# Adding the two parts of H by TensorE with two stacked unit matrices, and copying the sum by ScalarE, in a fused embedding and interaction kernel

## The reference, cut to what matters

```
# inp = e: [512, 32, 64]; W0: [128, 32*32], W1 and W2: [128, 64*32]
h = inp
for i, (W, b) in enumerate([(W0, b0), (W1, b1), (W2, b2)]):
    Wr = W.reshape(O, Hj, nf)
    nxt = einsum('bjk,bzk,ojz->bok', h, inp, Wr) + b[None, :, None]
    if i != n_layers - 1:
        h, o = nxt[:, :O // 2], nxt[:, O // 2:]
    else:
        o = nxt
    outs.append(o)
z = sum(concatenate(outs, axis=1), axis=2)
h = relu(concat([z, dense_ctx]) @ W_top1 + b_top1)
h = relu(h @ W_top2 + b_top2)
y = h @ W_top3
```

## Time and profile before

| | before |
|---|---|
| median of three executions | 665.0 us |
| the profiled execution's own time | 666.33 us |
| its span, first to last instruction | 664.6 us |
| mean granted TensorE clock | 0.977 of full speed |
| TensorE busy (matmuls / weight loads) | 627.3 us (94%) / 520.8 us (78%) |
| VectorE busy | 484.8 us (73%) |
| ScalarE busy | 213.1 us (32%) |
| GpSimd busy | 128.9 us (19%) |

### The profile page before, as it was taken

One profiled execution on the slowest core, in us unless ns is written; L12 is line 12 of the kernel. 1 busy time (PEld: TensorE's weight loads), 2 busy tenths in 40 slices (PEclk: granted clock), 3 DMA queues, 4 the chain that ended last, 5 costly groups with the idle time before them and its releaser, 6 DMA issues.

```text
span 664.6 us, 32262 instructions
## 1 busy us (share of the span) xinstructions
PE 627.3 (94%) x14488; PEld 520.8 (78%) x14488; DVE 484.8 (73%) x491; ACT 213.1 (32%) x351; POOL 128.9 (19%) x137
## 2 busy tenths in 40 slices
PE   5844899999999999999999999999999999999998
PEld 5833588888888888888888888888888888888773
DVE  4237788888888888888888888888888888851000
ACT  2330333444433333333333333333333333332012
POOL 7755044445443544100000000000000000000000
PEclk9686899999999999999999999999999999999999
DMA  5110011111111111100000000000000000002000
GB/s 180 30 28 17 14 24 28 28 25 32 26 25 24 29 26 27 20 15 13 12 12 12 12 12 12 12 12 12 12 12 12 12 12 12 12 18 65 11 1 0
DMA packets 31658, 14.87 MB, mean 22 GB/s; under 512 B 24177, under 2 KB 28897, under 8 KB 31378
## 3 DMA queue, kind: packets, MB, share of 16 engines
q1 hardware_dynamic: 27442, 10.26, 7.2%
q0 software_dynamic: 4192, 4.25, 2.9%
HBM read 8.03 MB, written 0.00 MB: 12 GB/s over the span
## 4 chain that ended last, share of the span: by engine, by line
PE 89%; POOL 5%; issue 3%; DVE 2%; DMA 1%; ACT 0%; DVEq 0%; POOLq 0%
PE psX L335 20%; PE psT L392 20%; PE psT L416 8%; PE psT L402 7%; PE psT L376 7%; PE psT L379 6%; POOL G_sb L239 5%; PE psX L379 4%; PE psX L376 4%; PE psX L346 3%; PE psX L466 2%; PE psX L355 1%; PE psX L273 1%; PE psT L480 1%; PE psX L496 1%
## 5 line engine op out<-in xcount | busy, mean ns | idle before, releaser
L392 PE MATMUL psT<-T_sb,W1d 64*64 64x256 f32 x1024 | 234.3, 379 | 0.0
L396 PE MATMUL psT<-T_sb,W1d 64*64 64x256 f32 x1024 | 234.3, 379 | 0.0
L402 PE MATMUL psT<-T_sb,W1d 64*64 64x256 f32 (+3 forms) x2048 | 205.3, 300 | 0.0
L684 DVE TENSOR_TENSOR prod<-X 128x1024 f32 (+4 forms) x202 | 170.7, 914 | 15.5 <-PE psT L379 15.3
L721 DVE STREAM_TRANSPOSE PT<-prod 128x4608 f32<-128x4608 f32 x32 | 159.0, 4969 | 0.0
L392 PEld LDWEIGHTS psT<-T_sb,W1d 64*64 64x64 f32 x1024 | 131.3, 133 | 27.8 <-issue 14.4
L335 PE MATMUL psX<-PT,W0T 32*64 32x256 f32 x4608 | 136.0, 382 | 12.5 <-DVE PT L721 9.1
L335 PEld LDWEIGHTS psX<-PT,W0T 32*64 32x64 f32 x4608 | 118.8, 134 | 32.9 <-issue 29.9
L416 PE MATMUL psT<-T_sb,W1d 64*64 64x64 f32 (+2 forms) x1536 | 141.7, 270 | 0.0
L396 PEld LDWEIGHTS psT<-T_sb,W1d 64*64 64x64 f32 x1024 | 131.3, 133 | 0.0
L402 PEld LDWEIGHTS psT<-T_sb,W1d 64*64 64x64 f32 x2048 | 123.6, 133 | 0.8
(11 more groups left out here) (78 smaller groups left out, 557.1 us busy)
## 6 DMA issues: line engine op xcount, KB each, us to landing
X<-T_sb SPq DMA_DIRECT2D x64, 64.0 KB, 2.0
kept<-grams SPq DMA_DIRECT2D x128, 16.5 KB
G_sb<-in_L_rec_W SPq DMA_DIRECT2D x2, 1024.0 KB, 4.8
E_q<-in_tbl,ids_g POOLq DMA_INDIRECT x96
prod<-in_W_top SPq DMA_DIRECT2D x2, 512.0 KB, 3.5
G_sb<-in_L_rec_W SPq DMA_DIRECT2D x1, 512.0 KB, 5.7
G_sb<-in_tbl,ids POOLq DMA_INDIRECT x32, 2.4
dT<-dT SPq DMA_DIRECT2D x3, 32.0 KB, 2.0
```

What stands on the lines that cost most here:

```text
L392: mm(psT[low, 0, 0:HF * SMP], W1d[low, HF + k, :], cross.rearrange("p v (z y) s -> p v z y s", y=HF)[:, :, :, k, :], start=start, stop=sto ...
L396: mm(psT[high, 0, 0:HF * SMP], W1d[low, k, :], T_flat[low, SMP * row:SMP * (row + HF)], start=start, stop=stop, tile_position=(0, C))
L402: last = mm(out[:, SMP * 4 * a:], W1d[high, HF * v + k, :], T_flat[high, SMP * (row + 4 * a):SMP * (row + HF)], start=start, stop=stop and ...
L684: return tt(out, x[:, :, z0:z0 + nz].unsqueeze(3).broadcast_to(shape), x[:, :, y0:y0 + ny].unsqueeze(2).broadcast_to(shape), ALU.mult)
```

## The change

TensorE makes 8 multiplies in place of the 16 transposes: the weights are all 128 rows by 128 columns of a tile of `H_sb`, the moving operand is `both`, two unit matrices of 64 x 64 one above the other. The product is the transposed sum of both parts, and lies in bank 0 of `psX`. ScalarE copies it to `H_T`, directly behind `h_copy`. VectorE's `ht_sum` is gone. VectorE makes `both` once at the start, and TensorE waits for it once. `b1_all` moves into a part of `G2_flat` that is free at that time.

```diff
+        both = sb("both", [P, C])
...
-        b1_all = sb("b1_all", [P, C])
...
+        b1_all = G2_flat[:, 7168:7168 + C]
...
             def h_transposes(m):
                 pe.wait_ge(h_evac, m + 1)
                 pe.sem_inc(turns, 1)
                 for t in range(TILES):
-                    for v in range(2):
-                        r = slice(C * v, C * v + C)
-                        last = nc.tensor.transpose(psX[:, v, C * t:C * t + C], H_sb[r, P * t:P * t + P], ident[r, r],
-                                                   tile_position=(C * v, 0))
+                    last = mm(psX[:, 0, C * t:C * t + C], H_sb[:, P * t:P * t + P], both[:, :], start=True, stop=True)
                 last.then_inc(h_tr, 1)
...
             h_matmuls(0)
+            pe.wait_ge(both_ready, 1)
             h_transposes(0)
...
+            def ht_copy(m):
+                act.wait_ge(h_tr, m + 1)
+                copy(H_T[:, :, :], psX[:, 0, :].rearrange("p (t o) -> p t o", o=C)).then_inc(ht_ready, 1)
...
             def step(n, lookups):
                 h_copy(n + 1)
+                ht_copy(n + 1)
...
             h_copy(0)
+            ht_copy(0)
             g0_copy(0)
...
             nc.vector.memset(kept[:, :, :, 0:NS:NS - 1], 0.0)
+            dve.wait_ge(identity, 2)
+            tt(both[:, :], ident[:, 0:C], ident[:, C:P], ALU.add).then_inc(both_ready, 1)
             nc.vector.memset(V_T[:, :, :], 0.0).then_inc(zeroed, 1)
...
-            def ht_sum(m):
-                dve.wait_ge(h_tr, m + 1)
-                nc.vector.tensor_reduce(H_T[:, :, :], psX[:, 0:2, :].rearrange("p v (t o) -> p t o v", o=C),
-                                        mybir.AxisListType.X, ALU.add).then_inc(ht_ready, 1)
...
             products(1, TILES)
-            ht_sum(0)
             dve.wait_ge(px_ready, 2)
...
                 products(e, dve.snap((n + 2) * TILES))
-                ht_sum(n + 1)
                 dve.wait_ge(px_ready, n + 3)
...
             t_copies(STEPS - 2)
-            ht_sum(STEPS - 1)
             add(STEPS - 2)
```

More of the change, by code:

```diff
@@ L138, in dlrm_tower @@
         ids0_in, idsg_in = sem("ids0_in"), sem("idsg_in")
-        identity = sem("identity")
+        identity, both_ready = sem("identity"), sem("both_ready")
         w0_sym = sem("w0_sym")
```

## The result

The changed kernel takes 700.8 us (median of four executions, 699.06 to 701.57) against 665.0 us before: the ratio is 1.054, with a 95% interval of 1.0509 to 1.0571. The forecast was 703.3 us, in a range of 694 to 714. The profiled execution took 699.06 us, its span is 697.3 us, 32.7 us above the span before.

A forecast was written before the change was run, and what follows sets the result against it. TensorE was taken to bound the steps. The terms 26.6 + 15.5 - 3.8 = +38.3 us on the profiled 666.33 gave 704.6, put on the median of the runs as 703.3 us; range 694 to 714.

The forecast's parts named there:

- The bound: In the steps TensorE is the bound; VectorE's sum is early by some 3.9 us, its transpose by 4.0 us.
- The rival by which VectorE sets the steps: VectorE's round is the longest, so removing 1.23 us from each of 32 gives 625.6 us; chance 0.01.
- 1. The multiplies: TensorE's stage at L346, paced like L469 at 0.121 us: 1.40 us per step without lookups, 1.29 with; 26.6 and 15.5 us.
- 2. ScalarE's copy at nothing: ScalarE's new 0.586 us copy falls into its idle time in each step, and nobody on TensorE or VectorE waits: cost 0.
- 3. The first step: Ahead of the loop VectorE's transpose no longer waits for its sum: 4.64 us gained, 0.81 lost before it, -3.8 in all.
- the drop of the clock goes with the stall: First step: without the 2.44 us wait at tile 5 the lower clock goes too; otherwise 2.2 us of gain are lost.
- The 0.77 us that the forecast left in place: A gap in L335 of the first step that nothing in the profile releases, expected to remain after the change.
- 4. Edits at nothing: Making `both` near the start is hidden by VectorE's wait for W0, and `b1_all` only changes its place: no cost.
- The one by which weight loads do not overlap in the whole array: At the stage no load runs beside the matmul before it: 15 loads of 0.203 us, total 743.9 us; chance 0.03.
- the one by which the moving columns alone set the pace: At L346 weights come in ahead of time, 16 pairs at 0.033 us each: 661.1 us, faster; chance 0.03.
- the half pace: Strides slow L469, and contiguous `both` runs at 0.066 us, the stage spans 0.99 us: 676.2 us; chance 0.07.

The follow-up runs named there:

- no_sum: The changed kernel with the 16 old transposes put back; ScalarE copies bank 0, so the second part of H is not added: 661.83 us, ratio 0.994.
- vector_copies: The changed kernel, but VectorE copies the sum to `H_T` at the place of its old reduction, and ScalarE does not: 703.18 us, ratio 1.0586.
- first_step_only: The kernel before, with multiplies by `both` and ScalarE's copy in the first step alone: 663.9 us, ratio 0.9979.
- held_first: The changed kernel, but VectorE's transpose ahead of the loop waits for `H_T` again: 703.10 us, against 701.35 for the unaltered changed kernel beside it.
- moving_32: The changed kernel with 32 instead of 64 moving columns in each multiply, half the outputs of H left out: 700.03 us, ratio 1.0531.

## Why the prediction was right, and where its terms were off

**The bound.** TensorE sets the steps, and VectorE's 1.23 us are worth nothing. This is shown by no_sum and vector_copies, in which the step without lookups stays within 0.01 us. The rival by which VectorE sets the steps is out.

**1. The multiplies.** This term carries the result, and its mechanism held: L469 was the right row to go by, and the loss is all in the stage. It was somewhat too high. The mean pace is 0.115 us and not 0.121, so 1.23 us and not 1.32; the exit is 430.40 - (428.48 + 1.725) = 0.195 us and not 0.235, so 0.04 more than before and not 0.08. Together 1.27, and the steps show 1.29 where I had 1.40. With lookups they show 1.16 (1.29 forecast); L275 starts right at the pace behind L346, as assumed. For the 31 steps the forecast was 42.1 us. Measured: 17 x 1.29 + 12 x 1.16 + 1.37 for the step between the two loops + 1.29 taken for the last stage, 38.5 us. L469's loads last 0.203 us and those of L346 0.192; why they do was not tried.

**2. ScalarE's copy at nothing.** Right: 2.65 us of idle time in front of it, and no wait for it on TensorE after the first step. With lookups the copies of looked up rows (L168, now L170) come behind it, and those steps grow by no more than the others.

**3. The first step.** The direction is right, the size of the gain was one profile's. The forecast was -3.8 us. From the two profiles first compared it is 5.09 us gained between L354 and L391, and 0.61 lost ahead of it, so -4.5, which would look like a confirmation and more. Over all profiles "first" goes from 16.57 (mean of three) to 13.84 (mean of two), -2.7 us. The direct comparison, first_step_only, gives -1.2 between medians and -0.3 to -2.5 by its interval, and held_first points the same way: 1.75 us lost without the new order, less the 0.61. So the gain is 1 to 3 us, and the forecast's 3.8 was too large. The measured 700.8 - 665.0 = 35.8 us (33.8 to 38.0 by the interval of the ratio) does not decide within that: 38.5 - 2.7 = 35.8 and 38.5 - 1.2 = 37.3 both fit.

What failed is the sentence that the drop of the clock goes with the stall, and the reading of 14.41 us as the length of this step. The wait is 2.44 us in all three profiles of before; the low stretch and the gap in L335 come and go from one execution to the next. The 0.77 us that the forecast left in place were 0 in one profile of the changed kernel and 0.65 in the other, and vector_copies had its long first step with the clock at full speed. What makes the gap is not shown.

**4. Edits at nothing.** The changed kernel's first copy of H stands at 61.97 us in one profile and 62.88 in the other, three profiles of before have 63.12, 62.85 and 62.79. Nothing there tells of `both` or of the new place of `b1_all`.

**The rivals.** The one by which weight loads do not overlap in the whole array is out: starts are 0.115 us apart with loads of 0.192. So is the one by which the moving columns alone set the pace, as moving_32 shows, and the half pace: with `both` contiguous it is 0.115 us and not 0.066, so the strides of L469 can explain at most the step from there to 0.121. The terms of the steps were too high by 3.6 us and the gain of the first step was too large by 1.1 to 2.6 us. These partly cancel, and the sum came out 2.5 us above the median. That it came so near is in part luck; the term that decides did not need any.

## What to carry to other kernels

An addition folded into TensorE is only free if TensorE has idle time there; look for who waits for whom before relieving an engine that has slack. A 32-bit transpose and a 32-bit multiply by a unit matrix do the same work here, but the multiply needs two pairs of load and matmul instead of one, and each pair is slower. For plain 32-bit multiplies with 64 moving columns or fewer, count the loaded columns and not the moving ones. Before you charge a one-off stretch at the start of a program to the wait in front of it, look at it in more than one profile.

## What the runs showed of the hardware that I had not expected

- The same wait of 2.44 us, at the same place of the same kernel, was followed by the lower clock in two profiles (0.69 and 0.68 over 70 to 75 us) and by the full clock in the third (1.00). Executions of the kernel before, 20 in one comparison, spread from 663.06 to 668.3 us.
- 16 plain pairs over the whole array and 32 in two row groups take the same 2.00 us. The transposes, with the same 128 loaded and 64 moving columns in the same two row groups, are far quicker: 0.066 us from one to the next in a row group, against 0.111.
- Transposes of 128 rows by 128 columns with 128 moving columns follow one another after (1.09 - 0.273) / 7 = 0.117 us, about as long as a plain pair with 64 or 32 moving columns (0.115, 0.113), though its load lasts 0.141 us and not 0.192.
